# Other PSUM banks for the last sequence's shared units and output projection, and one block for attention, shared experts and experts

## The reference, cut to what matters

```python
h = h + attention(layernorm(h))        # 16 heads of 64, windows of 128, 16 learned keys before them
flat = layernorm(h)                    # 2048 tokens
logits = flat @ gate_w                 # 16 experts, the best 2 for each token
...
idx = top_k(wm, 320)                   # the tokens of each expert, at most 320
y = (silu(flat[idx] @ w1) * (flat[idx] @ w3)) @ w2 * weight   # for each of 16 experts
shared = mean over 2 shared experts of swiglu(flat)           # for all tokens
out = h + scatter_add(y) + shared
```

## Time and profile before

| what | us |
|---|---|
| median of three runs | 2105.56 (2102.9 to 2107.07) |
| the profiled execution, its own time | 2102.53 |
| its span in the profile | 2100.7 |
| TensorE busy | 2037.0 (97%) |
| VectorE busy | 1299.0 (62%) |
| ScalarE busy | 1031.9 (49%) |
| GpSimd busy | 215.8 (10%) |
| last step of the encoder ends, attention begins | 1312.4 to 1313.7 |
| last sequence's step 1 begins (scores, L1112) | 1654.99 |
| shared stage ends, experts begin | 1868.8 to 1870.7 |

### The profile page before, as it was taken

The page is one execution under the profiler, slowest core; times in us unless marked ns, Lnnn a source line. Parts: engine busy times, 40 slices in busy tenths (PEclk is TensorE's granted clock), DMA queues, the critical chain, the costliest instruction groups (busy, mean ns, idle before and its releaser), DMA issues. The chain is left out here.

```text
span 2100.7 us, 42201 instructions
## 1 busy us (share of the span) xinstructions
PE 2037.0 (97%) x16462; PEld 1657.2 (79%) x16462; DVE 1299.0 (62%) x3344; ACT 1031.9 (49%) x3525; POOL 215.8 (10%) x251
## 2 busy tenths in 40 slices
PE   5899999999999999999999999899999999999998
PEld 4688888888888888888888877678788788877776
DVE  4676767676676776766767863767777646423322
ACT  3666656656566565666656552545445531111111
POOL 4000000000000000000000000000000000234444
PEclk9999999999999999999999999999999999999999
DMA  6000000100000400000000000500000100025542
GB/s 182 1 1 2 1 2 2 69 1 2 1 2 1 155 2 2 2 2 1 2 2 2 2 1 1 183 1 1 1 1 1 61 1 11 24 78 165 156 142 65
DMA packets 27203, 69.84 MB, mean 33 GB/s; under 512 B 9920, under 2 KB 17825, under 8 KB 23680
## 3 DMA queue, kind: packets, MB, share of 16 engines
q1 hardware_dynamic: 18432, 59.42, 8.4%
q0 software_dynamic: 6400, 5.63, 1.1%
q10 hardware_dynamic: 2176, 2.10, 0.3%
HBM read 61.16 MB, written 17.40 MB: 37 GB/s over the span
## 5 line engine op out<-in xcount | busy, mean ns | idle before, releaser
L547 ACT ACTIVATE probs<-bank,nmax 128x256 f32<-128x256 f32 x1024 | 474.4, 478 | 413.1 <-DVE nmax L716 413.1
L716 DVE TENSOR_REDUCE nmax<-bank 128x2 f32<-128x512 f32 x512 | 317.9, 683 | 208.6 <-PE bank L401 205.4
L414 PE MATMUL bank<-ident,probs 128*128 128x128 f32 x2048 | 271.9, 276 | 5.1 <-DVE pts L724 5.1
L414 PEld LDWEIGHTS bank<-ident,probs 128*128 128x128 f32 x2048 | 232.6, 141 | 39.7 <-DVE pts L724 22.5
L446 PE MATMUL bank<-yT,weights 128*128 128x256 f32 x1024 | 248.3, 386 | 0.9 <-ACT aT L570 0.9
L458 PE MATMUL bank<-weights,aT 128*128 128x256 f32 x1024 | 232.6, 380 | 1.3 <-DVE h L754 0.8
L547 ACT ACTIVATION_READ_ACCUMULATOR probs<-bank,nmax 128x1 f32 x1024 | 216.0, 211 | 0.0
L446 PEld LDWEIGHTS bank<-yT,weights 128*128 128x128 f32 x1024 | 184.5, 190 | 37.7 <-ACT aT L570 11.6
L458 PEld LDWEIGHTS bank<-weights,aT 128*128 128x128 f32 x1024 | 189.5, 190 | 25.3 <-DVE h L754 1.2
L724 DVE COPY pts<-bank 128x512 f32<-128x512 f32 x256 | 172.8, 675 | 38.6 <-PE bank L414 38.5
L556 ACT ACTIVATE pts<-bank 128x512 f32<-128x512 f32 x256 | 156.8, 612 | 21.4 <-PE bank L414 18.7
(11 more groups left out here) (218 smaller groups left out, 2935.4 us busy)
## 6 DMA issues: line engine op xcount, KB each, us to landing
wqkv<-in_experts SPq DMA_DIRECT2D x16, 1024.0 KB
weights<-in_wtok SPq DMA_DIRECT2D x4, 2048.0 KB, 19.0
wqkv<-in_experts SPq DMA_DIRECT2D x16, 512.0 KB
expert_rows<-xT_all SPq DMA_DIRECT2D x10, 546.0 KB, 16.5
xrows<-expert_rows SPq DMA_DIRECT2D x16, 273.0 KB
weights<-in_wtok SPq DMA_DIRECT2D x3, 1024.0 KB
wqkv<-in_wqkv SPq DMA_DIRECT2D x1, 3072.0 KB, 17.5
weights<-in_shared SPq DMA_DIRECT2D x1, 3072.0 KB, 10.8
```

The costliest lines, as they stand in the source:

```text
L414: last = pe.transpose(g[:, (NT * x + kb) * P:(NT * x + kb + 1) * P], p[:, x, kb * P:(kb + 1) * P], ident[:])
L547: last = nc.scalar.activation(probs[u % 8][:, x, :], g[:, x * S:(x + 1) * S], ACT.Exp, bias=nmax[j % 2][:, col:col + 1], accum_out=rsum[j ...
L716: nc.vector.tensor_reduce(nmax[j % 2][:, col:col + 2], g[:].rearrange("p (x s) -> p x s", x=2), AX.X, ALU.max, negate=True).then_inc(s_max, 1)
```

## The change

Three things are changed in the table of banks, and the second and third block become one.

- Place A goes to bank 2 instead of 7 in the steps after the last sequence (s = 8): units 8 and 12. At s = 7 it stays in bank 7.
- Place C goes to bank 5 instead of 7 where s is a sequence: units 5 and 7. Unit 10 (s = 8) stays in 7.
- ("wo", 6, 1), the second half of the output projection of the sequence before the last, goes to bank 5. The other seven stay in 7.
- `attention_and_shared` and `experts` get one block and one scope of semaphores. There is no barrier between them. In its place VectorE waits, before it opens bank b for the experts, until the last unit of the shared stage in that bank has been evicted (`bank_left`).

```diff
@@ attention_and_shared
-                for x, b in (("A", 7), ("B", 0)):
+                for x, b in (("A", 7 if seq(s) else 2), ("B", 0)):
                     if (s, c, x) in early:
                         use(upper(early[s, c, x]), b)
...
-                for x, b in (("C", 7), ("D", 2 if c == 0 else 7)):
-                    if (s, c, x) in early and x == "C":
-                        use(upper(early[s, c, x]), b)
+                if (s, c, "C") in early:
+                    use(upper(early[s, c, "C"]), 5 if seq(s) else 7)
...
                 if c == 1 and seq(s - 1):
-                    use(("wo", s - 1, 1), 7)
+                    use(("wo", s - 1, 1), 5 if s == B - 1 else 7)
...
-        block = ctx.enter_context(nc.Block(no_gpsimd_drain=True))
...
+        def bank_left(eng, b):
+            eng.wait_ge(s_free[b], sum(x == b for _, x in order) + 1)
+
+        return bank_left
@@ experts
-        block = ctx.enter_context(nc.Block(no_gpsimd_drain=True))
...
         def _(dve):
 
+
+            bank_left(dve, 6)
             for i in range(6):
+                bank_left(dve, i)
                 nc.vector.memset(scratch[:, i:i + 1], 0.0).then_inc(s_free[i], 1)
@@ build
+        block = ctx.enter_context(nc.Block(no_gpsimd_drain=True))
```

More of the change, by code:

```diff
@@ L842, in attention_and_shared @@
 def attention_and_shared(nc, io, h, ident, weights, wqkv, wout, norm, normab, gamma, pmk, w_yT, w_qT0, w_kT0,
-                         loads, XS, half_of):
+                         loads, XS, half_of, sem, block):
     T16 = B * NT
@@ L858, in attention_and_shared @@
         sb = lambda name, shape, dt=F32: ctx.enter_context(nc.sbuf_tensor(name, shape, dt))
-        sem = lambda name: ctx.enter_context(nc.semaphore(name))
         mask = sb("mask", [P, 1, KEYS2])
@@ L1758, in places, with experts @@
         sp.dma_start(self.rows[a][64:64 + CAP - full * P, full, D:], src[full * P:, D:]).then_inc(self.s_rows[a], 16)
-def experts(nc, io, ident, loads, half_of):
+def experts(nc, io, ident, loads, half_of, sem, block, bank_left):
     ctx = ExitStack()
@@ L2021, in build @@
         embed_and_encoder(nc, io, h, ident, weights, wqkv, wout, norm, normab, gamma, pmk, w_yT, w_qT0, w_kT0)
-        attention_and_shared(nc, io, h, ident, weights, wqkv, wout, norm, normab, gamma, pmk, w_yT, w_qT0, w_kT0,
-                             loads, XS, half_of)
-        experts(nc, io, ident, loads, half_of)
+        block = ctx.enter_context(nc.Block(no_gpsimd_drain=True))
+        bank_left = attention_and_shared(nc, io, h, ident, weights, wqkv, wout, norm, normab, gamma, pmk, w_yT, w_qT0, w_kT0,
+                                         loads, XS, half_of, sem, block)
+        experts(nc, io, ident, loads, half_of, sem, block, bank_left)
 def layout(x):
```

## The result

In the comparison that goes with this prediction the kernel after took 2090.41 us (median of 4 runs, 2087.28 to 2092.55), the kernel before 2105.61 (4 runs, 2102.9 to 2107.07): a ratio of 0.993 with an interval of 0.9915 to 0.9946. The forecast of 2097.2 had the sign right and the size too small: 15.2 us against 8.4, and the time lies under the range's lower end of 2092.5. The profiled execution of after took 2087.28, its span is 2085.5; it is the fastest of the four.

The account below looks back on a forecast made before the run. TensorE, busy 97% of the span, was taken as the bound, so only its waits could be won: 2.23 + 3.87 + 0.59 + 0.75 + 0.96 = 8.4 us, from the median 2105.56 to 2097.2; range 2092.5 to 2101.

Parts of the forecast that it names:

- ("wo", 6, 1) in bank 5: Step (7, 1): the output projection starts 0.11 us after the third turned part, at 1661.23 instead of 1663.46; 2.23 us.
- unit 5 in bank 5: Step (7, 2): `pv` starts at 1678.98 instead of 1682.85; 3.87 us, of which 1.59 from the clock staying at 2.4 GHz.
- unit 7 in bank 5: Behind the third part at 1692.10: `pv` follows at 1694.04 instead of 1694.63; 0.59 us.
- unit 8 in bank 2: No more wait for ScalarE's copy of x_T(6) in bank 7: 0.69 us plus some 0.06 of overlap; 0.75 us.
- the seam: From shared stage to experts: without the barrier VectorE's memset, and TensorE's first transpose, come 0.96 us earlier, at worst 0.41.
- The wait of 0.4 us for ScalarE's copy: Before `pv` in step (7, 2): one wait of 0.4 us for ScalarE's copy of the third part was expected.
- The count of six waits: From step (7, 1) to the first expert TensorE was said to wait in six places, 0.34 to 2.59 us each.
- four rivals: Low clock all the same (2098.8 us, 0.12), dear branch (2099.6, 0.06), ScalarE's chain (2102.3, 0.06), slower through bank 5 (2109.3, 0.04).
- wait for a bank-5 eviction: Sign of the slower rival: bank 5 becomes the narrow one, an eviction slips a whole step; 2109.3 us, chance 0.04.
- The dear branch: Rival at the seam: fetching the second stream without a barrier costs 1 to 2 us; gain about 6, 2099.6 us; chance 0.06.
- own range is 2094 to 2101: Range in us of the likeliest case, from runs of before spreading 2.7 below to 1.5 above their median.
- B: Theory of the experiments: the changed program as a whole makes the encoder faster, so all 15 us belong to the change.

Follow-up runs that it names:

- the second group's after: The kernel after, unchanged, run again beside other runs of before: 2094.01 us (5 runs), ratio 0.9961.
- the filler: Idle TensorE matmuls (6, 8 and 10) ahead of three encoder waits: in before 2098.3 us, 0.9984; in after 2088.96 us, 0.9943.
- the load edit: SyncE's weight loads at the encoder's start held until bias rows have landed: in after 2090.9 us, 0.9949; in before 2103.2 us, 1.001.

## Why the forecast was right and where it was not

**Right: mechanism and terms.** Read start to start, before minus after, in the first pair of profiles:

| step | forecast | measured |
|---|---|---|
| ("wo", 6, 1) in bank 5 | 2.23 | 2.23, and 0.12 up to the next third part |
| unit 5 in bank 5 | 3.87 | 3.85 |
| unit 7 in bank 5 | 0.59 | 0.60 |
| unit 8 in bank 2 | 0.75 | 0.95 |
| the seam | 0.96 | 1.01 |
| sum | 8.4 | 8.76 |

Unit 8 is the one term that was too small: I gave the overlap 0.06, and it was worth 0.26. The wait of 0.4 us for ScalarE's copy that was to replace unit 5's stall came (0.43), and so did the untouched 0.5 us. The count of six waits left out one, 0.4 us for VectorE's `keys`, which stands in both kernels. None of the four rivals came. No wait for a bank-5 eviction appeared, the seam's shorter stops left the clock at full speed in the nine profiles without a barrier, and ScalarE holds one step by 0.43 us only. The dear branch is refuted as well: the rule in the Trainium skill, "Runtime: NRT & Kernel Launch", Instruction fetch mechanics, that a branch away from the fetched code waits for memory, doesn't show as a cost here, with the memset starting where the eviction ends.

**Wrong: the base.** The step that failed is the one from the terms to a time: "Against its own time the profiled execution would come to 2102.53 - 8.4 = 2094.1", and then "I forecast the median: 2105.56 - 8.4". Both treat all that lies ahead of step (7, 1) as a constant. It isn't: attention's first scores came between 1308.0 and 1316.8 in the profiles of this study, for encoder code that is the same but for the edits shown. 5.04 of the 15.2 us lie there, and 1.48 behind it: from the first scores to step (7, 1) it is 341.0 to 341.8 us in the 6 profiles in which attention's first projection takes 7.1 us at the low clock, and 339.5 to 340.5 in the 12 in which it takes 5.4. The two sides of the first comparison drew opposite ends. The "own range is 2094 to 2101" took the spread of three runs of before, 4 us, for the spread of the kernel; over the whole study the unchanged kernel before ran from 2095.8 to 2107.1 (82 runs, median 2102.6) and after from 2087.1 to 2095.6 (16 runs, median 2092.3). The medians are 10.3 us apart, 0.5%; in the three groups with several runs of after the difference was 15.2, 8.7 and 10.8. Against these medians the miss of some 6.7 us splits in three: the base of 2105.56 was 2.9 too high, the runs of after drew 1.9 under their own median, and 1.9 are what 10.3 has over the forecast gain of 8.4. The draw isn't one of single executions only: all five runs of the second group's after (2093.05 to 2094.75) lie above all four of the first's. The later groups ran on four different chips; what sets a group's level isn't shown.

**Wrong, smaller: the clock after the 2.07 us wait.** I wrote that after it the clock "is 1.00" and that "a stop of this size falls on either side", but in the sum only unit 5's wait carries a price for it. It draws the lower level in 3 of 8 profiles at 1.7 us, so removing it is worth 0.6 us more on average; unit 5's term is 0.2 smaller on average by the one profile in 8 without a low clock. The seam's one case in nine adds 0.2. That brings the mean gain of the stretch from 8.8 to about 9.4 us (8.76 + 0.64 - 0.19 + 0.19). The 10.3 between the medians is not told from that: runs of one kernel lie up to 11 us apart, and the three groups' differences 6.5.

**What stays open.** Whether after gets the early encoder more often than before (2 of 4 profiles of the unchanged kernel, to 0 of 3), as B in a weaker form would have it, or by chance. The same goes for the low clock at attention's first projection, worth 1.7 us: 5 of 9 profiles with three blocks, 1 of 9 with one. B as stated is out: the same program has given 1308.6, 1315.2, 1308.1 and 1314.2. And the clock in the encoder goes with the time in both directions and obeys the filler, but what makes one execution draw the low level in the first place was not found. The landing of the bias row and GpSimd's meeting with VectorE don't decide it alone; in the unchanged kernels the two profiles with the row added by 26.30 us are the two early ones, and the five with it at 30.20 or later the late ones, so they may be part of it.

## What to carry to other kernels

A stall that follows a full bank is worth its wait, plus what the passes behind it ran too slowly, minus the wait for the next engine: worked out from start times that way, five terms came to 8.4 us where 8.8 was measured. The sum is a difference, though, and the time that it is taken from is one draw. Before giving a range, ask which stretches that the change doesn't touch hold waits of 2 to 3 us on an engine with a granted clock, and widen it by what they cost; and compare the start of the changed stretch in both traces before crediting the change with anything.

## What the runs showed of the hardware

- Waits of TensorE of nearly one length fall on either side of the clock's fall: 2.07 us drew 1.2 GHz in 3 of 8 profiles, 2.6 us in 7 of 8. A longer wait isn't a surer one elsewhere: at attention's start, waits of 2.5 to 3.7 us drew it in 6 of 18, and the six longest (3.29 to 3.71) never. The same program gains or loses by it 1.7 us at the projections and 1.2 to 1.6 at unit 5's eight passes (3.15 to 3.62 us instead of 1.99). Matmuls whose result is thrown away, put into three waits of 1.4 to 2.6 us, bought 3.4 us for the kernel before (0.9984 [0.9975, 0.9993]).
- Small operations of VectorE stood still while GpSimd added tiles in SBUF: two on `h` took 4.67 us instead of 0.73, from 27.41 to 32.08, and GpSimd's three additions end at 28.20 + 3.71 = 31.91. The Trainium skill, "SBUF — State Buffer", SBUF: two separate sides, speaks of a port pair that the two engines share and that is locked for a whole instruction; here it stayed closed for three in a row. Whether it costs the kernel anything isn't settled: keeping the two apart, with the load edit, took 2.3 us off before and nothing that could be told off after.
